# Where a graph-attention kernel makes its one-hot matrices: TensorE products of codes, or ScalarE and VectorE

## The reference

```python
q = x @ Wq + bq;  k = x @ Wk + bk;  v = x @ Wv + bv          # each [6250, 8, 16]
scores = sum(q[dst] * k[src], -1) / 4 + (edge_attr @ We + be)  # [200000, 8]
e = exp(scores - segment_max(scores, dst)[dst])
probs = e / (segment_sum(e, dst) + 1e-10)[dst]
agg = segment_sum(probs[:, :, None] * v[src], dst)
out = layernorm(x + agg @ Wo + bo)
```

## Time and profile before

| | |
|---|---|
| median of 3 runs | 2024.04 us |
| lowest, highest | 2020.06, 2025.88 us |
| span of the profiled execution | 2449.4 us (425 us above the median) |
| the profiled execution's own time | only its span is given |
| mean granted TensorE clock | 0.786 of full |
| DMA moved in the span | 288.11 MB, mean 118 GB/s |

### The profile page before, as it was taken

One profiled execution on the slowest core, in us unless ns is written; L12 is line 12 of the kernel. 1 busy time (PEld: TensorE's weight loads), 2 busy tenths in 40 slices (PEclk: granted clock), 3 DMA queues, 4 the chain that ended last, 5 costly groups with the idle time before them and its releaser, 6 DMA issues.

```text
span 2449.4 us, 25231 instructions
## 1 busy us (share of the span) xinstructions
PE 1545.6 (63%) x6655; PEld 1051.5 (43%) x6655; DVE 1370.8 (56%) x3214; ACT 454.6 (19%) x1496; POOL 1496.0 (61%) x1572
## 2 busy tenths in 40 slices
PE   5354576657665757566656666566766666666566
PEld 4233454435343434444444444344444444444344
DVE  4254575656555655555655656555555555556556
ACT  1011121212121211111111212111211212111112
POOL 4736546666666666666666666666666666666661
PEclk7677788868778777877887887877878778788878
DMA  6423334343334334343434343434334343434331
GB/s 248 160 84 105 94 101 130 107 123 115 118 117 130 109 108 130 107 131 108 129 108 128 111 129 108 128 108 125 112 113 127 110 128 111 126 111 127 108 106 31
DMA packets 115143, 288.11 MB, mean 118 GB/s; under 512 B 45909, under 2 KB 53856, under 8 KB 107960
## 3 DMA queue, kind: packets, MB, share of 16 engines
q0 software_dynamic: 74624, 203.26, 28.3%
q1 hardware_dynamic: 37628, 76.52, 9.4%
q10 hardware_dynamic: 2748, 6.69, 0.7%
HBM read 274.69 MB, written 11.67 MB: 117 GB/s over the span
## 4 chain that ended last, share of the span: by engine, by line
PE 40%; issue 25%; another core or an unknown queue 14%; DVE 10%; POOL 9%; DMA 1%; ACT 1%; DVEq 0%; ACTq 0%; POOLq 0%
PE ps_q L1230 14%; PE ps_a L1266 11%; POOL kv_buf L523 9%; PE ps_e L1242 2%; PE ps_t L1216 2%; PE ps_t L1210 2%; DVE prod L850 1%; DVE score L860 1%; DMA kv_buf<-kv_table,src_i 1%; PE ps_s L1294 1%; DVE wv L870 1%; PE ps_a L1319 1%; DVE run_fwd L912 1%; PE ps_a L1320 1%
## 5 line engine op out<-in xcount | busy, mean ns | idle before, releaser
L523 POOL DMA_INDIRECT kv_buf<-kv_table,src_i x1536 | 1465.6, 954 | 899.6 <-issue 407.5
L1230 PE MATMUL ps_q<-q_blk,hots 128*128 128x256 f32 x1564 | 566.4, 497 | 553.8 <-issue 553.6
L1230 PEld LDWEIGHTS ps_q<-q_blk,hots 128*128 128x128 f32 x1564 | 351.9, 246 | 677.7 <-issue 625.2
L1266 PE MATMUL ps_a<-wv,hots 128*128 128x272 f32 x1564 | 559.9, 490 | 8.5 <-issue 5.6
L613 ACT ACTIVATE hots<-ps_t 128x512 f32<-128x512 f32 x377 | 225.1, 597 | 1784.8 <-remote 1035.1
L850 DVE TENSOR_TENSOR prod<-ps_q,kv_buf 128x512 f32<-128x512 f32 (+1 forms) x392 | 268.7, 685 | 497.8 <-remote 322.7
L870 DVE TENSOR_TENSOR wv<-kv_buf,ps_w 128x512 f32<-128x512 f32 (+1 forms) x392 | 266.3, 679 | 238.8 <-remote 179.5
L1266 PEld LDWEIGHTS ps_a<-wv,hots 128*128 128x128 f32 x1564 | 335.4, 238 | 61.0 <-issue 10.4
L860 DVE TENSOR_REDUCE score<-prod 128x32 f32<-128x512 f32 (+1 forms) x392 | 267.2, 682 | 7.9 <-issue 0.2
L930 DVE TENSOR_TENSOR_SCAN ps_s<-seq_far,seq_left,ps_s 8x512 f32<-8x512 f32 x57 | 72.7, 1275 | 188.0 <-remote 155.0
L1309 PE MATMUL ps_a<-sums_sb,carry_from 128*1 128x136 f32 x112 | 28.0, 342 | 195.2 <-DVE sums_sb L982 154.8
(11 more groups left out here) (157 smaller groups left out, 1398.1 us busy)
## 6 DMA issues: line engine op xcount, KB each, us to landing
edge_f<-in_edge_blk SPq DMA_DIRECT2D x55, 1024.0 KB
kv_buf<-kv_table,src_i POOLq DMA_INDIRECT x1536
kv_table<-kv_buf ACTq DMA_DIRECT2D x12, 512.0 KB, 3.2
xt_blk<-in_x_t SPq DMA_DIRECT2D x114, 32.0 KB
out<-y_out SPq DMA_DIRECT2D x114, 32.0 KB
kv_buf<-in_x_perm SPq DMA_DIRECT2D x5, 512.0 KB
codes<-code_table SPq DMA_DIRECT2D x108, 10.5 KB
code_table<-kv_buf SPq DMA_DIRECT2D x1, 1344.0 KB
```

Source lines behind the costliest of these rows:

```text
L523: pool.indirect_dma_start(kv_buf[:, b % NBUF, t, :], None, kv_table, bass.IndirectOffsetOnAxis(ap=src_i[:, column:column + 1], axis=0)).th ...
L1230: one = pe.matmul(ps_q[q % 2][:, k * 2 * D:(k + 1) * 2 * D], hots[:, (v - 1) % 2, 0, k * P:(k + 1) * P], q_blk[:, b % QBUF, :], start=True ...
L1266: one = pe.matmul(sums(b), hots[:, (v - 1) % 2, 1, k * P:(k + 1) * P], wv[:, q % 2, 2 * k:2 * k + 2, :].rearrange("p j w -> p (j w)"), sta ...
```

## The change

The products of codes go, with the code rows, their table, their loads and the setup of both codes. In their place:

- SP loads the destinations themselves, as int32, each half's row of 1792 broadcast to 64 partitions (`load_dst`, two loads of 448 KB a block, two block buffers `dst_bc`).
- ACT makes the one-hots by node in two passes of 256 columns a step: gap = |dst - node| (`gaps_to_nodes`, int32 in, three buffers) and then relu(1 - gap) (`hots_by_node`, four buffers), three and two slots ahead of the spread.
- DVE makes the one-hots by edge, one comparison of 256 columns a step (`hots_by_edge`), just before `weigh` of the same step, from `iota_n` and the destinations relative to the window, `rel`, both in SBUF (three buffers).
- The bank `ps_t` becomes a third bank of the spread (SPREADS = 3), and `wv` has three buffers (WVBUF = 3).
- POOL's held wait on `s_matched` goes; the waits on `s_byedge` and `s_summed` stay. All the new one-hots lie in the space of `x_first`, which is free after block 0's setup.

```diff
+    NHOT, NGAP, EHOT, WVBUF, SPREADS = 4, 3, 3, 3, 3
...
+            def load_dst(b):
+                if b >= DBUF:
+                    sync.wait_ge(s_gap, FIRST[b - DBUF + 1])
                 n = HALF[b] * P
                 for j in range(2):
                     row = 2 * b + j
-                    sync.dma_start(codes[j * KNOWN:(j + 1) * KNOWN, b % CBUF, 0:n], code_table[:, row * ROW:row * ROW + n]
-                                   ).then_inc(s_code[b % CBUF], 16)
+                    sync.dma_start(dst_bc[j * W:(j + 1) * W, b % DBUF, 0:n], dst_row[row:row + 1, 0:n].to_broadcast([W, n])
+                                   ).then_inc(s_dstbc[b % DBUF], 16)
...
                         if b >= HELD and t == t0:
                             pool.wait_ge(s_byedge, q - AHEAD + 1)
-                        if b >= HELD and t == t0 + 1:
-                            pool.wait_ge(s_matched, HOTS_TO[slot_of(q - AHEAD)])
...
-            def copy_hots(v):
-                act.wait_ge(s_matched, HOTS_TO[v])
...
+            def gaps_to_nodes(q):
+                b, g = STEPS[q]
+                t0, t1 = STEP[b][g]
+                if g == 0:
+                    act.wait_ge(s_dstbc[b % DBUF], 32 * (b // DBUF + 1))
+                if q >= NGAP:
+                    act.wait_ge(s_near, q - NGAP + 1)
+                act.activation(gaps[:, q % NGAP, 0:(t1 - t0) * W], dst_bc[:, b % DBUF, t0 * W:t1 * W], ACT.Abs,
+                               bias=neg_node[:, b:b + 1]).then_inc(s_gap, 1)
+
+            def hots_by_node(q):
+                b, g = STEPS[q]
+                t0, t1 = STEP[b][g]
+                act.wait_ge(s_gap, q + 1)
+                if q >= NHOT:
+                    act.wait_ge(s_byedge, q - NHOT + 1)
+                act.activation(near_hots[:, q % NHOT, 0:(t1 - t0) * W], gaps[:, q % NGAP, 0:(t1 - t0) * W], ACT.Relu,
+                               bias=1.0, scale=-1.0).then_inc(s_near, 1)
...
+            def hots_by_edge(q):
+                b, g = STEPS[q]
+                t0, t1 = STEP[b][g]
+                pairs = (t1 - t0) // 2
+                if q >= EHOT:
+                    dve.wait_ge(s_summed, q - EHOT + 1)
+                dve.tensor_tensor(
+                    edge_hots[:, q % EHOT, 0:pairs * P].rearrange("p (k j n) -> p k j n", j=2, n=W),
+                    iota_n[:, 0:W].rearrange("p (a b n) -> p a b n", a=1, b=1).to_broadcast([P, pairs, 2, W]),
+                    rel[:, columns(b, 0, TILES[b])].rearrange("p (j t a) -> p t j a", j=2, a=1)[:, t0 // 2:t1 // 2]
+                    .to_broadcast([P, pairs, 2, W]), ALU.is_equal)
...
                     if step_in(v - SLOT - LAG) is not None:
+                        hots_by_edge(step_in(v - SLOT - LAG))
                         weigh(step_in(v - SLOT - LAG))
...
             def spread_q(v):
-                pe.wait_ge(s_copied, HOTS_TO[v - 1])
-                if q >= 2:
-                    pe.wait_ge(s_product, q - 1)
+                pe.wait_ge(s_near, q + 1)
+                if q >= SPREADS:
+                    pe.wait_ge(s_product, q - SPREADS + 1)
...
-                    if v in HOTS_TO:
-                        match(v)
```

More of the change, by code:

```diff
@@ L89, in graph_attention @@
     FIRST_HALVES = [(g, h) for g in range(GS[0]) for h in range(2)]
-    assert all(t1 - t0 == QUAD for t0, t1 in STEP[0]) and NB >= 4 and len(GROUPS) >= KNOWN
+    assert all(t1 - t0 == QUAD for t0, t1 in STEP[0]) and NB >= 4
     HALVES_TO = [sum(1 for j, _ in HALVES if j < k) for k in range(len(GROUPS) + 1)]
@@ L121, in graph_attention @@
         kv_buf = sb("kv_buf", [P, NBUF, T, KV])
[L122 to L126, removed]
+        dst_bc = sb("dst_bc", [P, DBUF, ROW], I32)
+        neg_n = sb("neg_n", [P, 1])
+        neg_node = sb("neg_node", [P, NB])
         edge_f = sb("edge_f", [2 * EF, 2, EPAIRS * P])
@@ L219, in graph_attention @@
         g_q = prod[:, 0, 0:D]
-        ps_t = ps("ps_t", [P, 2 * QUAD * W])
-        ps_q = [ps(f"ps_q{i}", [P, 512]) for i in range(2)]
+        ps_t = ps("ps_t", [P, 512])
+        ps_q = [ps(f"ps_q{i}", [P, 512]) for i in range(2)] + [ps_t]
         ps_w, ps_e = ps("ps_w", [P, 512]), ps("ps_e", [P, 512])
@@ L275, in graph_attention @@
         SETUP = numbered("ident zero", "iotas", "ident")
[L276 to L279, removed]
+        s_node = sem("s_node")
+        NODE = numbered("numbers", "of blocks")
         s_const = sem("s_const")
-        CONST = numbered("ones", "zeros", "codes", "iota", "bias kv", "scaled")
+        CONST = numbered("ones", "zeros", "iota", "bias kv", "scaled")
         s_win = sem("s_win")
@@ L287, in graph_attention @@
         s_found = sem("s_found")
-        FOUND = numbered("node codes", "spread", "falls")
+        FOUND = numbered("spread", "falls")
         s_spread = sem("s_spread")
@@ L680, in _ @@
                     copy_q(b)
-                copy_hots(-1)
-                for v in SLOTS:
-                    if v in HOTS_TO:
-                        copy_hots(v)
+                act.wait_ge(s_node, NODE["of blocks"])
+                for v in range(-3, SLOTS[-1]):
+                    if step_in(v + 3) is not None:
+                        gaps_to_nodes(step_in(v + 3))
+                    if step_in(v + 2) is not None:
+                        hots_by_node(step_in(v + 2))
                     if chain(v, 4) is not None:
@@ L727, in _ @@
             dve.memset(eps_c[:, :], LN_EPS)
-            for k, less in enumerate((0.0, -32.0, -16.0)):
-                dve.memset(less_c[:, k:k + 1], less)
             dve.memset(q_blk[:, :, :], 0.0)
@@ L796, in _ @@
             dve.tensor_copy(base_bc[:, :], base_ps).then_inc(s_win, 1)
+            dve.wait_ge(s_node, NODE["numbers"])
+            for j in range(2):
+                own = slice(j * W, (j + 1) * W)
+                one = dve.tensor_scalar(neg_node[own, :], base_ps[own, j::2], -1.0, neg_n[own, :], ALU.mult, ALU.add)
+            one.then_inc(s_node, 1)
             dve.tensor_scalar(carry_from[:, 1::2], step_ps[:, 1::2], part[:, 0:1], None, ALU.is_equal)
@@ L828, in _ @@
                 own = columns(b, j * HALF[b], (j + 1) * HALF[b])
-                one = dve.tensor_scalar(neg_rel[:, own], dst_i[:, own], -1.0, base_bc[:, i:i + 1], ALU.mult, ALU.add)
+                one = dve.tensor_scalar(rel[:, own], dst_i[:, own], base_bc[:, i:i + 1], None, ALU.subtract)
             one.then_inc(s_win, 1)
@@ L1326, in _ @@
                     project_q(b)
-                match(-1)
                 for v in SLOTS:
```

166 lines of the change are left out of this document (32 added, 134 removed).

## The result

The changed kernel takes **2037.4 us** in the median of five runs (2031.9 to 2042.6), the kernel before 2024.0 (2019.1 to 2026.4) beside it: ratio **1.0071 [1.0056, 1.0086]**, 11 to 17 us slower. The forecast was 2036.

A forecast was written before the change was run, and what follows sets the result against it. POOL's back-to-back gathers were taken to bound the kernel, their path 2018 us against a 2024 us median. 2024 - 6 (TensorE, buffers) + 18 (comparisons holding gathers), other terms zero, gave 2036 us, range 2030 to 2065.

The forecast's parts named there:

- POOL's path sets the time: POOL issues gathers back to back from about 41 to 1975 us; its path sums to 2018 us, all else hides.
- I take these stalls as part of the profiled execution alone.: Waits in the 2449 us profile, with several engines idle together, were assumed absent from the timed runs.
- VectorE against POOL, +18: The new comparisons, with both inputs in SBUF, hold up POOL's gathers: +18 us, ends 0 and 168.
- TensorE and the third buffers, -6: Dropping code products and adding buffers loosens POOL's coupling to TensorE: -6 us, ends 0 and -108.
- Start 0: At the kernel's start, removing the setup of codes gains nothing, as POOL's gathers of x run past it until 40.6 us.
- End 0: In some ten last steps without gathers, work lost and gained nearly cancels: zero, ends -4 and +4 us.
- ScalarE: One 597 ns copy replaced by two passes of about 383 ns: +0.17 us a step, 66 us in all, hidden.
- Transfers 0: The 52 MB of destination loads arrive before ScalarE needs them, hidden by 8 us and the spread's buffers: zero.
- 1: Rival: the comparison mostly falls between gathers' starts, losing a third of 18 us or less: 2022 us; chance 0.30.
- rival 2: The comparison lies over a gather's moment in most steps, costing 0.21 us in 384 steps: 2104 us; chance 0.08.
- Rival 3: TensorE was late for POOL in the timed runs too, so lighter work pays: 1970 to 2010 us; chance 0.16.
- rival 4: Destination loads take twice as long and arrive late, costing 2 us a block: 2134 us; chance 0.04.

The follow-up runs named there:

- second profile: The kernel before, unchanged, profiled again on a chip where it takes about 2024 us: one run 2028.01 us, span 2026.2 us.
- a1: The changed kernel with the comparison's second input read from PSUM instead of SBUF, its values not the wanted ones: 2025.08 us, 0.9998 of the kernel before.
- b1: The kernel before with only the comparison of 256 columns added ahead of each `weigh`, its result unused: 2035.24 us, 1.0045 of the kernel before.
- c1: The changed kernel with the comparison's node numbers copied once to PSUM and read there, same one-hots: 2027.02 us, 1.0015 of the kernel before.
- d1: The kernel before with its memset of codes in 16 pieces and one input of two maxima per block in PSUM: 2019.49 us, 0.9995 of the kernel before.
- a4: The changed kernel with destinations loaded for the first two blocks only and reused later: 2037.33 us, 1.0057 of the kernel before.

## Why the prediction was right, and where it wasn't

The prediction was 2036 and slower, the result 2037.4. The mechanism of the price was right; that the number came out within 1.4 us is luck, since two terms of it were off by 6 us in opposite directions. By its steps:

- **POOL's path sets the time.** Right: in the nine profiles of the table the waits over the regular gap are 3.2 to 7.5 us of some 2030. The sum of 2018 came from a profile with stalls and falls 8 us short of the span of the second profile: the first gather from the table starts at 43.2 where 40.6 was taken (the wait for the table was left out), the tail is 50.4 for 43.6, waits over the regular gap add 3.2, and a gather with its gap is 0.951 + 0.305 = 1.256 for 1.259, which gives 4.6 back.
- **"I take these stalls as part of the profiled execution alone."** Wrong as put. They belong to a chip or its state, and there the timed runs have them too. The reading worked only because the times shown were from elsewhere. What ends these waits stays open.
- **VectorE against POOL, +18.** The mechanism is shown: taking away the second SBUF input alone gives 12.7 us back (a1), adding the comparison alone costs 8.2 (b1), and c1 with the same one-hots has the short gathers again. The size was over: 12.0 us in the profile, some 12 in the runs. The mis-sized step is the rate of 0.107 of an operation's time. It laid the whole 14 us of excess on five operations; counted in that same trace, the gathers that meet those five lose 6.8 us (5.2 in the second profile), a rate of 0.05 or 0.04, which would have given +7 to +9. The rest of the 14 lay on operations with a scalar column (2.5), on the setup (2.0) and on differences under 15 ns (2.8). The comparison's own rate is 12.0/162.1 = 0.074. The moment at which a gather is exposed was put at 0.19 us of age. Behind a scan it is 0.19 (the gather ends 0.75 us after the scan), behind a comparison 0.13. The Trainium skill (SBUF — State Buffer, Who interferes with whom) has the rule on two SBUF inputs, and a1 and c1 agree with it: both with one input in PSUM, 951 ns. Its rule that the second comer is blocked for the whole instruction agrees with the first two pairs above, where the comparison holds the gather to its end. The other way round the trace doesn't agree: a comparison that starts with or just behind a gather lasts up to 0.48 us and doesn't wait out the gather's 0.945.
- **TensorE and the third buffers, -6.** Nothing: POOL's waits over the regular were 3.2 us before and are 4.6 and 7.5 after. a1 and c1, the change without its price, stand at 0.9998 and 1.0015. The 6 us weren't coupling but an error of the path sum. The relief was also smaller than the 255 us of the two rows: in that same trace the code products cover 188 us, and 55 of these stand alone. In the second profile it is 64 alone, of which the slower other products took 45, and the rest lay on no path.
- **Start 0.** It was -2.7. The memset of the codes, not read in the first profile, isn't the cause, though it held POOL's first gather and the change has no such memset: without that hold, in d1, POOL just waits longer for the table. The table sets the start. Its last part leaves VectorE at 34.3 us in the kernel before, 35.6 in d1 and 32.1 in the changed kernel, and the first gather from it follows 8.2 to 8.9 us later in all three. In the kernel before, the chain that ends at that gather leads over ScalarE's code passes (L578 and L584, to 12.1 us); the changed kernel has no such passes. No run takes them out alone, so that they are the 2.7 us isn't shown. **End 0:** 49.5 and 48.1 against 50.4, within the bound of 4.
- **VectorE 0.43 us each, hidden.** 416 ns, 162 us, hidden (a1). **ScalarE** was mis-sized: the first pass, from int32 and with a bias by partition, takes 503 ns (no run separates the two), the second 404, where 383 was taken for both, so by the rows a step gained 0.31 us, not 0.17. The page shows only 67 us more, since the passes overlap: in the changed kernel's timeline the second starts some 0.1 us before the first ends. Hidden. **Transfers 0:** right (a4).
- **Rivals.** 1 and 2 were the two ends of one question, how often a comparison meets a gather. The answer, 99 of 392, lies between: rival 2 wanted over one in three. The moment is covered in 140 steps, over one in three, but a comparison that starts with the gather takes nothing from it, and each of the 99 costs 0.12 us, not 0.21. Rival 3 is refuted by the second profile, rival 4 by a4.

So the sum was 2024 - 6 + 18, and measured it reads 2024 - 0 + 12 with 1 or 2 us to spare: two errors of 6 us against each other, both inside the range. With the rate that its own trace gave, the sum would have read 2025 to 2027.

## What to carry to other kernels

When the bounding engine is GpSimd issuing indirect DMAs, ask of each operation moved to VectorE where its inputs lie, not how long it takes: the same 162 us of comparison cost 12 us with two SBUF inputs and none with one in PSUM. Relief for an engine that isn't on the bounding path is worth nothing, so look first at that path's waits over its regular gap; here they were 3 us. And take a profile in the same state as the times before laying the sum on it.

## What the runs showed of the hardware

- A memset of 128 x 3584 f32 by VectorE (3.04 us) held an indirect DMA of GpSimd: 3.90 us instead of 1.11, until 1.07 us after the memset's end. In pieces of 224 columns it held nothing that shows.
- A VectorE comparison with a pointer to a scalar in SBUF (64 columns, 271 ns) holds gathers as well: 97 of the gathers, 3.7 us lost. (One input there is a full SBUF operand, the other the scalar column.)
- A gather is exposed about 0.13 us after its start (changed kernel): all 80 comparisons with two SBUF inputs that began over 0.03 us ahead of it and ended later than 0.15 us into it held it, and cost it what was left of them. Of the 34 that began from 0.03 us before to 0.05 us after its start, 30 cost nothing. Of the 22 that began 0.06 to 0.13 us after it, 15 cost 1.0 us together; most of these gathers end 0.48 us behind the comparison, not 0.82, so it isn't one moment for all.
